# Second layer's context products in four bursts of 13 units a pair, where they stood in five of 10 or 11

## The reference, cut to what matters

```python
scores_t = jnp.einsum('bhsd,bhtd->bhst', q, k_t) * attn_scale
probs_t = jax.nn.softmax(scores_t, axis=-1)
text_out = jnp.einsum('bhst,bhtd->bhsd', probs_t, v_t)
qsem = jnp.einsum('bhst,bte->bhse', probs_t, text_ehs)   # 256 columns a head
qsem = _l2norm(qsem)
sem = jnp.einsum('bhse,bne->bhsn', qsem, ip_n)
fused = attn_scores + SEM_SCALE * sem
probs_ip = softmax(fused) * spatial_mask
out = (text_out + merge(probs_ip @ v_ip)) @ W_out + b_out + residual
```

## Time and profile before

| | |
|---|---|
| timed runs, median | 1537.2 us |
| profiled execution, its own time | 1539.36 us |
| its span from the first to the last instruction | 1537.6 us |
| mean granted clock of TensorE | 0.971 of full speed |
| PE busy | 95% of the span |
| ACT, DVE busy | 70%, 73% |
| from 640 us to 1500 us | the second layer's units |

### The profile page before, as it was taken

How to read it: one execution, slowest core, us unless ns; L and a number is a source line. 1 busy time by engine, 2 the same in 40 slices (tenths; PEclk the granted TensorE clock), 3 DMA queues, 4 the chain that set the end, 5 groups by cost and what they waited for, 6 DMA issues and landing times. The chain is left out here.

```text
span 1537.6 us, 32818 instructions
## 1 busy us (share of the span) xinstructions
PE 1463.5 (95%) x12886; PEld 912.5 (59%) x12886; DVE 1122.0 (73%) x1602; ACT 1069.2 (70%) x1974; POOL 189.1 (12%) x363
## 2 busy tenths in 40 slices
PE   7888969999999999999999999999999999999998
PEld 4455523333333333477777777777777777777776
DVE  5777778887787877876767777777767777777742
ACT  2445548877877877876767778777777777787762
POOL 4563300000101101100001000000000000000000
PEclk9899869999999999899999999999999999999997
DMA  5156851111221211110010111000100011001000
GB/s 154 59 170 184 231 119 51 51 51 42 56 55 44 65 45 47 47 26 22 18 26 23 30 26 27 23 19 24 27 23 21 22 26 26 21 20 26 7 1 18
DMA packets 82839, 75.91 MB, mean 49 GB/s; under 512 B 28544, under 2 KB 70900, under 8 KB 82692
## 3 DMA queue, kind: packets, MB, share of 16 engines
q1 hardware_dynamic: 82692, 73.87, 18.1%
HBM read 47.73 MB, written 26.09 MB: 48 GB/s over the span
## 5 line engine op out<-in xcount | busy, mean ns | idle before, releaser
L1389 DVE TENSOR_TENSOR whole<-late,whole 128x1024 f16<-128x1024 f32 (+1 forms) x280 | 319.9, 1142 | 101.6 <-ACT whole L1243 98.4
L1129 PE MATMUL ps_v<-eh,whole 128*128 128x269 f16 x1040 | 292.5, 281 | 0.0
L1374 DVE TENSOR_REDUCE mx<-ps_y 128x2 f32<-128x800 f32 (+2 forms) x227 | 223.7, 986 | 93.3 <-PE ps_y L1051 92.9
L1129 PE MATMUL ps_n<-eh,whole 128*128 128x269 f16 x1040 | 291.4, 280 | 0.0
L1243 ACT CAST whole<-late 128x1024 f16<-128x1024 f32 (+1 forms) x280 | 275.6, 984 | 8.9
L1132 PE MATMUL ps_v<-eh,whole 128*128 128x269 f16 x960 | 268.7, 280 | 0.0
L1131 PE MATMUL ps_v<-el,whole 128*128 128x269 f16 x960 | 268.6, 280 | 0.0
L1132 PE MATMUL ps_n<-eh,whole 128*128 128x269 f16 x960 | 268.1, 279 | 0.0
L1131 PE MATMUL ps_n<-el,whole 128*128 128x269 f16 x960 | 267.9, 279 | 0.0
L1374 DVE TENSOR_REDUCE mx<-ps_x 128x2 f32<-128x800 f32 (+2 forms) x198 | 195.3, 986 | 79.2 <-PE ps_x L1051 79.0
L1374 DVE TENSOR_REDUCE mx<-ps_t 128x2 f32<-128x800 f32 (+2 forms) x215 | 211.3, 983 | 32.2 <-PE ps_t L1051 31.9
(11 more groups left out here) (435 smaller groups left out, 2093.1 us busy)
## 6 DMA issues: line engine op xcount, KB each, us to landing
e<-in_ctx SPq DMA_DIRECT2D x4, 1536.0 KB
kb<-k_parts SPq DMA_DIRECT2D x80, 74.9 KB
kb<-k_parts SPq DMA_DIRECT2D x80, 74.7 KB
k_parts<-kp SPq DMA_DIRECT2D x12, 400.0 KB
vb<-v_cols SPq DMA_DIRECT2D x40, 117.0 KB, 2.1
v_cols<-late SPq DMA_DIRECT2D x4, 1040.0 KB, 11.4
late<-v_cols SPq DMA_DIRECT2D x40, 104.0 KB, 2.0
qb<-q_parts SPq DMA_DIRECT2D x160, 25.0 KB
```

Of the source, the lines that this page charges most:

```text
L1129: pe.matmul(ps, hi, eh, start=(t == 0), stop=False)
L1374: nc.vector.tensor_reduce(mx[:, pair % 2, c, :], bank("max", pair, c)[:, :, 0:w], AX.X, ALU.max).then_inc(chunk_max, 1)
L1389: nc.vector.tensor_tensor(pl[s % 2][:, t0:t0 + w, :], ring[:, turn % EXPS, 0:w], ph[s % 2][:, t0:t0 + w, :], ALU.subtract).then_inc(low_do ...
```

## The change

The burst table goes from five entries to four: 13 units behind fills 3, 7, 11 and 14, so that each burst holds one `hh` whole. The gaps then hold fills 0 to 3, 4 to 7, 8 to 11 and 12 to 14. The third `unit_out` moves on ACT from behind exponential 5 to behind exponential 6.

```diff
-UNITS_AFTER = {2: (0, 10), 5: (10, 21), 8: (21, 31), 11: (31, 42), 14: (42, 52)}
-UNIT_OUT_AFTER = {2: 0, 4: 1, 5: 2}
+UNITS_AFTER = {3: (0, 13), 7: (13, 26), 11: (26, 39), 14: (39, 52)}
+UNIT_OUT_AFTER = {2: 0, 4: 1, 6: 2}
```

## The result

The changed kernel takes 1641.38 us (median of 4 runs, 1636.97 to 1643.74) against 1538.33 us before: ratio 1.0668, interval 1.0645 to 1.0691. In a second series of 5 runs it was 1.0665 (1.0651 to 1.0679). It is slower by 102 to 103 us; forecast were 97.8. The profiled execution took 1636.97 us with a span of 1635.2, where the prediction gave 1637.2 for it. That this is so close is partly luck, as the next lengths show.

A forecast was written before the change was run, and what follows sets the result against it. The prediction took PE, without waits in the second layer, as the bound: -7.4 (boundaries) + 98.0 (waits) + 4.2 (table loads) + 3 (clock) = +97.8 us on 1537.2 gave 1635.0 us, range 1624 to 1652.

The forecast's parts named there:

- The fourth fill waits for the bank of the first: In three of four gaps a step, the fourth fill waits for the first fill's exponential: 98.0 us in all.
- Price of the first gap: Fourth fill 1.68 us behind the first instead of 0.62: 1.06 us in each of 38 steps, 40.3 us.
- Price of the second gap: Fourth fill 1.51 us behind the first instead of 0.62: 0.89 us in each of 37 steps, 32.9 us.
- Price of the third gap: Fourth fill 1.51 us behind the first instead of 0.84: 0.67 us in each of 37 steps, 24.8 us.
- Three longer waits: At the heads of steps 54, 64 and 74, ACT's table load adds 1.40 us to the wait: 4.2 us.
- One boundary less: Second layer, 39 steps: one change between fills and unit products fewer, 0.19 us each, -7.4 us.
- The clock: PE's clock falls at two of the three long waits in the second layer, costing 3 us.
- What stays hidden: Second layer: other work of ACT and DVE, moved `unit_out`, turned maxima and low parts cost PE nothing: 0 us.
- A step of 24.2 us: Second layer: a step lengthens from 21.8 us by 2.6 for waits, less 0.2 for the boundary.
- the clock in ordinary gaps: Rival: the clock falls in ordinary gaps too, 57 us more (1692) or 168 more (1803); chance 0.07.
- a late engine: Rival: late ACT or DVE lengthens one wait a step by a cast, +40 us, 1675; chance 0.04.
- an earlier release: Rival: the fourth fill's bank is free sooner, waits some 0.3 us smaller each, 1601 us; chance 0.03.

The follow-up runs named there:

- e2: Kernel before with the first burst behind fill 3 instead of fill 2, so one gap has four fills, bursts as before: 1.029, +44.6 us.
- e6: Kernel before with the second burst behind fill 6 instead of 5, so a four-fill gap starts with a maxima fill that DVE empties: 1.023, +35.4 us.
- e4: Changed kernel with ACT's fourth `unit_out` behind the first exponential and PE's wait for the keys' load ahead of fill 4: 1.0585 against the kernel before.
- e1: Kernel before with the last burst cut in two, behind fills 13 and 14, one boundary more a step: 1.0049, +7.5 us.
- e5: Changed kernel with copies for the first three batches' square roots, so without six table loads in the second layer: 1.06 against the kernel before.

## Why the prediction was right, point by point

- **PE has no waits in the second layer, so its losses move the end one for one.** Right: +100.4 us from first to last unit, +102 to 103 in the time.
- **The fourth fill waits for the bank of the first.** Right, and shown by e2 and e6 (one gap, either engine) and by e4 (moving ACT's order moves PE).
- **Price of the first gap, 1.06 us.** Right: the fourth fill stood at 1.68 us as worked out. The count was one too high. In step 41 PE has other work (`turn_result`, L1073) between fills 1 and 2 and still runs at the lower clock, so that the fourth fill comes 2.97 us behind the first (632.98 to 635.95) and doesn't wait. 37 x 1.06 = 39.2, where I had 40.3. The seven gaps with a stage cost about the same: they grew by 8.4 us in all, where seven ordinary first gaps grow by 8.8.
- **Price of the second gap, 0.89.** Too small by 0.09: 1.60, not 1.51. The term that was mis-sized is the release (from the exponential's end to the fill's start), for which I took 0.05 from a product with one wait. The fill has a second semaphore, the keys' load; without it the 1.51 came out. 37 x 0.98 = 36.3, where I had 32.9.
- **Price of the third gap, 0.67.** Right: 1.51 us. 24.8.
- **Three longer waits, 4.2 us.** Right: 3.09 - 1.68 = 1.41 each.
- **One boundary less, -7.4 us.** Right within its error: e1 measured +7.5 (5.5 to 9.5) for one more, 8.1 in the trace.
- **The clock, 3 us for two falls.** Right for the profiles: 2.9 us by the starts of the products behind them. The place was less sure than I wrote: the falls skip one of the three long waits in each profile of the changed kernel, and e4 had its only one elsewhere. That there were two was a choice between nothing and three, not worked out.
- **What stays hidden.** Right: no wait for DVE, the copies of `unit_out` or the low parts; ACT idles for 2.19 us ahead of the second gap.
- **A step of 24.2 us.** From step 54 to step 74 it took (1452.14 - 961.55)/20 = 24.5 us: the second gap's 0.09 more, and the long waits and clock falls (about 0.2 a step here), which the sum has apart.

The terms with the measured prices: 39.2 + 36.3 + 24.8 + 4.2 + 2.9 - 8.1 = 99.3 us, against 100.4 from first to last unit. The 1.1 us between them is as much as 0.01 us of reading in each of the 111 waits. Of the rivals, the clock in ordinary gaps would have shown in the changed kernel's profiles and in e5, a late engine in PE's waits, an earlier release in the 1.68; none did, but for the one clock fall of e4.

The time of 1641.4 us is 6.4 above the forecast. The median before, which came out at 1538.3 and not at 1537.2, is 1.1 of it. The second layer is 2.6: +3.4 for the second gap, -1.1 for the wait too many, -0.7 for the boundary, -0.1 for the clock, and the 1.1 that stay open. The last 2.7 lie outside the second layer, where the sum has no term, and are within the uncertainty of the ratio (3.5 us either way in this series, 2 in the second).

## What to carry to other kernels

Where PE is the bound and its results leave through n banks in turn, a run of fills without other work between should not be longer than n, unless an emptying is shorter than the fills that follow it. Here fill n + 1 waited for a whole emptying (1.0 us on ACT or DVE, 1.4 to 1.7 from fill to fill), however idle the emptying engine was. A table that sets how work is interleaved has to be read against the number of banks first, and against the number of boundaries (0.2 us) only then: here one boundary saved bought three waits of 0.7 to 1.1 us.

## What the runs showed of the hardware that I had not expected

- A product that waits for two semaphores started 0.15 us behind the end of the exponential it waited for (1020.89 to 1021.04), where one that waits for the exponential alone started 0.05 behind. With the other wait, for the keys' load, placed a few fills earlier, the 0.1 was gone (37 times, 3 us), and PE lost nothing at the new place, so that semaphore had long been up. The trace of the changed kernel shows how the two waits are laid out. The one for the exponential is an instruction of its own on PE's weight-load side (`PEldq`), and the weight load follows at 1021.01:

```profile
L1031 PEldq EVENT_SEMAPHORE  x1: 51/51/51, 1020.9 to 1020.9; - x1
```

- Going from a unit product (128 rows and 128 columns) to the turned maxima (128 rows, 2 columns) takes 0.21 us from start to start, as going to a fill of half the rows does.
- In the four profiles of the changed kernel, eight falls of the clock came behind twelve waits of 2.3 us, and in e2's two behind three. e4 had none behind three waits of 2.1 us and one behind a wait of 0.52 us, and e5 had none behind 111 waits of up to 1.1 us. A fall cost 1.2 to 1.7 us, since PE then ran 12 to 16 unit products at 1.2 GHz, about 0.22 us apart.
